# A decoder layer on one core: the feed-forward stage in seven products, its second matmul summed in PSUM

## The reference, cut to what matters

```
x = x + attention(layernorm(x), ...)         # block-sparse cache, 32 heads
x = x + cross_attention(layernorm(x), ...)   # 32 heads
x = x + ffn(layernorm(x), W1, b1, W2, b2)

def ffn(x, W1, b1, W2, b2):                  # x: 1024 x 512
    h = gelu(x @ W1 + b1)                    # W1: 512 x 2048, tanh form
    y = h @ W2                               # W2: 2048 x 512
    y = nan_to_num(y, nan=0, posinf=0, neginf=0)
    return y + b2
```

## Time and profile before

| | |
|---|---|
| median of three runs | 2126.07 us |
| the profiled execution, its span | 2129.9 us, 2128.0 us |
| granted clock over the span | 0.991 |
| feed-forward stretch (1935 to 2112 us), PE busy | 176.4 of 177 us |
| the same stretch, DVE, ACT, POOL | 127.5, 57.5, 44.6 us |

### The profile page before, as it was taken

The page is one execution under the profiler, slowest core; times in us unless marked ns, Lnnn a source line. Parts: engine busy times, 40 slices in busy tenths (PEclk is TensorE's granted clock), DMA queues, the critical chain, the costliest instruction groups (busy, mean ns, idle before and its releaser), DMA issues.

```text
span 2128.0 us, 33928 instructions
## 1 busy us (share of the span) xinstructions
PE 2076.8 (98%) x11620; PEld 1789.8 (84%) x11620; DVE 1500.9 (71%) x2365; ACT 1017.3 (48%) x2232; POOL 548.7 (26%) x428
## 2 busy tenths in 40 slices
PE   8999999999999999999899999999999999999996
PEld 7888888888888888888788888888888888877885
DVE  6777777777777777777766666666666666677776
...
DMA packets 44162, 76.90 MB, mean 36 GB/s; under 512 B 7378, under 2 KB 13650, under 8 KB 43602
## 3 DMA queue, kind: packets, MB, share of 16 engines
...
...
## 4 chain that ended last, share of the span: by engine, by line
PE 88%; DVE 6%; issue 3%; ACT 2%; DMA 1%; SPq 0%; DVEq 0%; ACTq 0%
PE bank L1087 22%; PE bank L1089 22%; PE bank L1088 22%; PE bank L1156 9%; PE bank L1202 6%; PE bank L1355 1%; PE bank L1354 1%; PE bank L1270 1%; PE bank L1271 1%; PE bank L1329 1%; DVE negmax L872 1%; DVE V_lo L866 1%; DVE xn L802 1%; DVE pT_lo L910 1%; DVE q_lo L904 1%
## 5 line engine op out<-in xcount | busy, mean ns | idle before, releaser
L882 DVE SCALAR_TENSOR_TENSOR xacc<-bank,rinv,xacc 128x512 f32<-128x512 f32 x512 | 375.7, 745 | 71.2 <-PE bank L1089 71.1
L481 ACT ACTIVATE pT_hi<-bank 128x512 fp32r<-128x512 f32 x320 | 190.8, 597 | 202.3 <-PE bank L1202 202.0
L872 DVE TENSOR_REDUCE negmax<-bank 128x1 f32<-128x640 f32 x256 | 210.2, 821 | 36.9 <-PE bank L1156 29.6
L535 ACT ACTIVATE prob<-bank,negmax 128x640 f32<-128x640 f32 x256 | 202.6, 791 | 66.2 <-DVE negmax L872 66.2
L910 DVE TENSOR_TENSOR pT_lo<-bank,pT_hi 128x512 fp32r<-128x512 f32 x320 | 217.5, 680 | 2.4 <-ACT pT_hi L481 2.4
L1202 PE MATMUL bank<-ident,prob 128*128 128x128 f32 x1280 | 191.3, 272 | 0.0
L1202 PEld LDWEIGHTS bank<-ident,prob 128*128 128x128 f32 x1280 | 159.2, 140 | 18.6
L378 POOL TENSOR_TENSOR wo_lo<-wo_raw,wo_hi 128x512 fp32r<-128x512 f32 x32 | 41.4, 1293 | 430.8 <-ACT wo_hi L481 430.8
L628 ACT ACTIVATE xprob<-xscore,negmax 128x128 f32<-128x128 f32 x256 | 99.5, 391 | 96.2 <-DVE negmax L963 96.2
L1087 PE MATMUL bank<-xwv_hi,cT_hi 128*128 128x256 f32 x512 | 143.4, 280 | 1.4 <-DVE xV_lo L930 1.4
L1088 PE MATMUL bank<-xwv_lo,cT_hi 128*128 128x256 f32 x512 | 143.1, 280 | 0.0
...
## 6 DMA issues: line engine op xcount, KB each, us to landing
wq_raw<-in_wq SPq DMA_DIRECT2D x32, 256.0 KB, 2.6
wo_raw<-in_wo SPq DMA_DIRECT2D x32, 256.0 KB, 2.6
xwv_raw<-in_xwv SPq DMA_DIRECT2D x16, 512.0 KB, 3.5
xwk_raw<-in_xwk SPq DMA_DIRECT2D x32, 256.0 KB, 3.5
xwq_raw<-in_xwq SPq DMA_DIRECT2D x32, 256.0 KB, 3.4
xwo_raw<-in_xwo SPq DMA_DIRECT2D x32, 256.0 KB, 2.6
w_raw<-in_w SPq DMA_DIRECT2D x32, 256.0 KB, 2.6
xacc<-in_x SPq DMA_DIRECT2D x8, 256.0 KB, 4.9
```

What stands on the lines that cost most here:

```text
L481: return s.activation(dst, src, ACT.Copy)
L535: s.activation(prob[:, slot, i, :].rearrange("p (a t) -> p a t", a=2), S_bank[i % 2], ACT.Exp, bias=negmax[:, slot, i:i + 1], scale=1.0, a ...
L872: v.tensor_reduce(negmax[:, slot, i:i + 1], S_bank[i % 2], mybir.AxisListType.XY, ALU.max, negate=True).then_inc(a["max"], 1)
L882: v.scalar_tensor_tensor(xacc[:, 4 * half + i, :], M, rinv[:, k, i:i + 1], xacc[:, 4 * half + i, :], ALU.mult, ALU.add).then_inc(sems["y"], 1)
```

## The change

**W1 by seven products.** The 512 inputs and the 1024 tokens are each cut in halves, W1's output blocks are taken in pairs (g, 8 groups: block 2g "first", 2g+1 "second"), and the 2 x 2 x 2 block product is made with seven products (P1 to P7) and sums of operands in place of eight. One product is 2 x 3 = 6 matmuls of 512 columns. P1 and P2 need only the first half of the tokens (`xB[0]`, `xB[1]`) and W1 itself (`we`, the early weights) and give, added, the hidden block 2g of the first half (c11). The other five need sums of the x quarters (`xS`, made on DVE in `xf`) and of the W1 quarters (`wl`, the late weights: four additions on POOL, `late_sums`; the five high parts in one copy of 1280 columns on ACT, `late_hi`; their low parts in one subtraction on DVE, `late_lo`). The results are combined on DVE: u2, u3, u4, then c12, c21, c22. `part` holds P1 (`p1_copy` on ACT). P1 and P2 run four groups ahead of the rest; groups 1 to 3 have them on banks 2 and 3, the others on 0 and 1.

**W2 by half.** For the first token half W2's products of all 16 blocks are summed in four PSUM banks (`y0`; 12 matmuls each, in whole or in two parts FIRST and LAST, in the order Y_ORDER). The second half's hidden values stay in `hid1` (16 x 512), and after the last group W2 is loaded once more (`again`, four buffers), split (`again_hi` on ACT; `again_lo` on DVE, every third on POOL), and the four tiles of the second half are done one after the other, each summing 16 x 3 matmuls in one bank. `yacc` is gone.

**Around it.** b2 is added to `xacc` by POOL after its last split of W2; `finish` makes the finite test and the sum on DVE straight from PSUM. W2's low parts are on DVE but for the first two. The first eight matmuls use only high parts. All loops are written out. The W1 and W2 semaphores reuse those of earlier stages (f_after). The buffers lie at fixed addresses.

```diff
@@ SP
+            def late_weights(g):
+                if g >= 2:
+                    sp.wait_ge(f["wlhi"], f0["wlhi"] + g - 1)
+                    sp.wait_ge(f["wllo"], f0["wllo"] + g - 1)
+                sp.dma_start(wl_f[g % 2][:, 0:4].rearrange("p (a s) c n -> p a (s c) n", a=2),
+                             w1[2 * g:2 * g + 2].rearrange("a p c n -> p a c n")).then_inc(s_wlraw[g % 2], 16)
+            def again(n):
+                if n >= 4:
+                    sp.wait_ge(f["ahi"], f0["ahi"] + n - 3)
+                    if (n - 4) % 3 == 2:
+                        sp.wait_ge(f["alo2"], f0["alo2"] + (n - 4) // 3 + 1)
+                    else:
+                        sp.wait_ge(f["alo"], f0["alo"] + n - 4 - (n - 4) // 3 + 1)
+                sp.dma_start(w2_again[:, n % 4], w2[n]).then_inc(s_x[n % 4], 16)
...
+            for g in range(NG):
+                for s_ in (7 + 2 * g, 8 + 2 * g):
+                    if s_ < NF:
+                        second(s_)
+                if g + 5 < NG:
+                    early(g + 5)
+                if g + 2 < NG:
+                    late_weights(g + 2)
+                if g == 4:
+                    sp.wait_ge(f["P2"], f0["P2"] + NG)
+                    for n in range(4):
+                        again(n)
+            for n in range(4, NF):
+                again(n)
@@ POOL
-            g.memset(yacc[:, :, :], 0.0).then_inc(s_y0, 1)
...
             pool.wait_ge(s_b, 16)
+            pool.wait_ge(L[3, "xn"], B)
+            for n in range(2, NF, 3):
+                pool.wait_ge(f["ahi"], f0["ahi"] + n + 1)
+                g.tensor_tensor(w2all_lo[:, n], w2_again[:, n % 4], w2all_hi[:, n], ALU.subtract)                 .then_inc(f["alo2"], 1)
             for b in range(B):
-                pool.wait_ge(L[3, "xn"], b + 1)
-                g.tensor_tensor(xacc[:, b, :], xacc[:, b, :], b2_sb[:, :], ALU.add).then_inc(s_xb, 1)
...
+                bias(b)
@@ ACT
+            for g in range(NG):
+                if g + 1 < NG:
+                    late_hi(g + 1)
+                for s_ in (5 + 2 * g, 6 + 2 * g):
+                    if s_ < NF:
+                        second_hi(s_)
+                if g + 4 < NG:
+                    p1_copy(g + 4)
+                if g + 1 == NG:
+                    hidden_late(g)
+                hidden_second(g, "c22", "g22", 2 * g + 1, late[:, 2])
+                if g + 4 < NG:
+                    hidden_early(g + 4)
+                if g + 5 < NG:
+                    early_hi(g + 5)
+                hidden_second(g, "c12", "g12", 2 * g, late[:, 1])
+                if g + 1 < NG:
+                    hidden_late(g)
@@ DVE
+            for g in range(NG - 1):
+                if g >= 4:
+                    late_lo(g + 1)
+                u2(g)
+                u4(g)
+                if g < 4:
+                    late_lo(g + 1)
+                u3(g)
+                c22(g)
+                for s_ in (5 + 2 * g, 6 + 2 * g):
+                    if s_ < NF:
+                        second_lo(s_)
+                if g + 4 < NG:
+                    c11(g + 4)
+                    h_lo(HALF_S[g + 4])
+                c12(g)
+                c21(g)
+                h_lo(LATE_S[g])
...
+            def finish(b, y):
+                if b >= 2:
+                    dve.wait_ge(f["fin"], f0["fin"] + b - 1)
+                v.tensor_scalar(finite[:, b % 2], y, 0.0, 0.0, ALU.mult, ALU.is_equal).then_inc(f["finite"], 1)
+                if b == 0:
+                    dve.wait_ge(s_xb, B)
+                v.tensor_tensor(ysum[:, b % 2], y, xacc[:, b, :], ALU.add).then_inc(f["sum"], 1)
+                dve.wait_ge(f["finite"], f0["finite"] + b + 1)
+                dve.wait_ge(f["sum"], f0["sum"] + b + 1)
+                v.copy_predicated(xacc[:, b, :], finite[:, b % 2], ysum[:, b % 2]).then_inc(f["fin"], 1)
...
+            for q in range(4):
+                hid1_lo_split(1, q)
+            for b in range(4):
+                finish(b, Y_bank[b])
+            for q in range(4):
+                hid1_lo_split(2, q)
+            dve.wait_ge(f["y1"], f0["y1"] + 1)
+            finish(4, Y1_bank[0])
...
@@ PE
+            for g in range(4):
+                fill = 3 if g == 0 else LATE_S[g - 1]
+                p6(g)
+                y0(fill, FIRST)
+                p5(g)
+                p1(g + 4)
+                p7(g)
+                p2(g + 4)
+                p3(g)
+                y0(fill, LAST)
+                p4(g)
+                y0(HALF_S[g + 4], EVERY)
+            p6(4)
+            for g in range(4, NG - 1):
+                p5(g)
+                p7(g)
+                y0(LATE_S[g - 1], FIRST)
+                p3(g)
+                p6(g + 1)
+                y0(LATE_S[g - 1], LAST)
+                p4(g)
...
+            for t_ in range(4):
+                for n in range(NF):
+                    if n % 4 == 0:
+                        pe.wait_ge(f["g1lo"], f0["g1lo"] + 4 * t_ + n // 4 + 1)
...
+                    last = mm3(Y1_bank[t_], [z[:, t_ % 2, n, :] for z in (hid1_hi, hid1_lo)],
+                               [z[:, n, :] for z in (w2all_hi, w2all_lo)], n == 0, n == NF - 1)
+                last.then_inc(f["y1"], 1)
```

More of the change, by code:

```diff
@@ L714, in _ @@
             ln_sqrt(3, 1)
[L715 removed]
+            for b in range(4):
+                x_first(b)
             ln_sqrt(3, 2)
[L718 to L724 removed]
@@ L742, in _ @@
-            f_step(0, 0)
-            with act.Fori(0, 6) as it:
-                for u in range(1, 5):
-                    f_step(it, u)
-            for u in range(1, 8):
-                f_step(6, u)
+            act.wait_ge(s_b1, 16 * NF)
+            s.activation(nrm[:, 4, 0:1], nrm[:, 1, 0:1], ACT.Gelu_apprx_tanh, bias=b1_sb[:, 0:1], scale=1.0)
+            late_hi(0)
+            p1_copy(0)
+            early_hi(3)
+            p1_copy(1)
+            hidden_early(0)
+            x_second(4)
@@ L1081, in _ @@
+            dve.wait_ge(f["y1"], f0["y1"] + 1)
+            finish(4, Y1_bank[0])
+            for q in range(4):
+                hid1_lo_split(3, q)
+            for b in range(5, B):
+                dve.wait_ge(f["y1"], f0["y1"] + b - 3)
+                finish(b, Y1_bank[b - 4])
         @block.tensor
@@ new lines, in y0 @@
+            def y0(s_, tiles):
+                if 0 in tiles:
+                    pe.wait_ge(f["hlo"], f0["hlo"] + s_ + 1)
+                    pe.wait_ge(f["w2lo"], f0["w2lo"] + s_ + 1)
+                for i in tiles:
+                    last = mm3(Y_bank[i], [z[:, s_ % 2, i * P:(i + 1) * P] for z in (hid_hi, hid_lo)],
+                               [z[:, s_ % 4, :] for z in (w2_hi, w2_lo)], s_ == 0, s_ == NF - 1)
+                if 3 in tiles:
+                    last.then_inc(f["y0"], 1)
```

630 lines of the change are left out of this document (468 added, 162 removed), and 3 rows, old and new, of the table f_after.

## The result

| | before | after |
|---|---|---|
| median, first comparison (four runs each) | 2126.21 | 2139.77 (2134.93 to 2143.48) |
| median, second comparison | 2127.46 | 2137.86 (2136.7 to 2140.96) |
| profiled execution, span | 2128.0 | 2141.5 |

The change is slower: ratio 1.0061, interval 1.0046 to 1.0077; the second time 1.0053, 1.0039 to 1.0068. The forecast was 2129 and the range ended at 2138; the second median lies just inside it, and the eight executions together have a median of 2139.2.

A forecast was written before the change was run, and what follows sets the result against it. The feed-forward stage was taken to run at PE's matmul rate. First product 1923.5, 168.0 of matmuls, waits, 3.2 of clock and a 5.3 tail summed to 2131.0, put as 2129 on the median; range 2112 to 2138.

The forecast's parts named there:

- the wait before tile 2: Second half of W2: tile 2's split stands on DVE behind finish and POOL's b2 adds; PE waits 7.0 us.
- lock: DVE and POOL block each other on shared ports; tile 1's splits and b2 adds add up, making tile 2's wait 8.1.
- P3's waits of 3 in groups 5 and 6 and 1 at group 7: PE waits for c22 before P3: 3.5 lost in groups 5 and 6, 1.0 in 7; groups 4 to 7 sum 9.7.
- the tail: After the last matmul, finish of one tile only: 5.3 us instead of 15.9.
- the first product: Head: PE's first product starts at 1923.5, 4.3 us earlier than before.
- Groups 0 to 3. Only P3 waits.: Groups 0 to 3: PE waits only at P3, 0.36 us each, 1.4 in all.
- none of over 0.5 in groups 1 to 3: Sign: no PE wait before P3 of over 0.5 us in groups 1 to 3.
- Group 4 loses 1.1.: Group 4: PE loses 1.1 us because POOL's sums come late behind the W1 load, as in group 5.
- The second half of W2: W2 reload through four buffers: PE ends tile 0 4.1 us late, then 0.5 for tile 1's first split.
- Clock. I take two falls: Two falls of PE's clock, one at tile 2 and one at group 5 or 6: 3.2 us (0 to 11).
- the 8 that I had named as a sign of being wrong: Sign: the prediction is wrong if the clock is low over more than 8 us.
- Rival 1: Clock falls at each long wait (head, groups 5 and 6, reload, tile 2): five falls, 11.0 us, 2137, slower; chance 0.20.

The follow-up runs named there:

- e6: Changed kernel with ACT's split of the early weights behind the two gelus of the late units instead of ahead: 2135.79 us.
- e10: Changed kernel with SP issuing each group's early and late weight loads ahead of the two W2 rows instead of behind: 2131.64 us.
- ep10: Changed kernel with e10's SP order, and PE doing all four W2 tiles ahead of P3 in groups 4 to 6: 2125.89 us.
- e4: Changed kernel with eight buffers instead of four for the second pass over W2: 2133.78 us.
- best2: Changed kernel with edits of e1, e2, e4, e6 and ep10, plus ACT's group 2 `p1_copy` ahead of `x_second(6)`: 2112.56 us.
- best3: best2 with POOL adding b2 ahead of the second pass over W2, and DVE making all sixteen `again_lo`: 2108.27 us.
- e0_again: The changed kernel run once more with no edit: 2137.86 us.
- e12: Changed kernel with the edits of e1 and e2 together: 2120.45 us.
- e1: Changed kernel with DVE splitting tile 2 of the second half before the finish of the first four tiles: 2130.36 us.
- e2: Changed kernel with DVE's split of the next late weights behind c22 instead of ahead of u2 in groups 4 to 6: 2128.38 us.
- e5: Changed kernel with filler matmuls on PE in the waits before P3 of groups 4 to 6 and before tile 2: 2133.89 us.
- e7: Changed kernel with POOL adding b2 ahead of its five W2 splits instead of behind them: 2129.45 us.

## Why the prediction was wrong

**What held.** The rate of the matmuls, the wait before tile 2 with its chain and its lock, P3's waits of 3 in groups 5 and 6 and 1 at group 7 (2.98, 3.03, 0.78), and the tail. Two sizes fit better than they deserve: the first product (1923.63 for 1923.5) came up to 3.8 us earlier in other executions, and the wait before tile 2 (6.73 for 7.0) was about 5.5 in seven. Of the lock, rows 11 do not show that "DVE began first": POOL's start is listed 0.01 us ahead. That POOL's adds stretch DVE's splits is shown by 6.88 against 2.49 us. The mechanism, in-order programs turning PE's saved work into waits, is shown: each wait went when the instruction in front of its releaser was moved, by what the timeline said.

**"Groups 0 to 3. Only P3 waits."** This step failed, by 4.4 us, and the sign "none of over 0.5 in groups 1 to 3" did too (1.23 and 1.51). P3 itself lost 0.27 in each of these groups, near the 0.36 forecast; what I had put at nothing is PE's wait for `hidden_lo`. It stands behind ACT's gelus, these behind ACT's split of the early weights, and that behind their load. I counted engine work and took each load as issued when its buffer is free. It is issued when SP's program comes to it, and that stood behind loads that wait for DVE. e6 (4.5 to 0.8 us in groups 1 to 3), e10 (none of these waits in groups 1 to 3) and ep10 (0.2 lost in each group) show it.

**"Group 4 loses 1.1."** It lost 2.75, from the same cause: with SP's new order alone the wait is gone. I had seen this for group 5 ("+0.6") and priced only the landing, 3.5, where 4.8 was the median.

**"The second half of W2", 4.1 and 0.5.** Mis-sized by 2.6. The round trip of four buffers was right as a mechanism (e4 saved 4.1), but with loads at 3.3 instead of 2.6, and I used the lock for tile 1 only. It is in tile 0 as well, since POOL splits every third row there: best2 loses 5.1 us in tile 0 with eight buffers and POOL's splits, best3 0.2 without these.

**"Clock. I take two falls", 3.2.** There were four in one execution and five in the other, 32 and 40 slow matmuls, 6.2 and 7.8 us. At 0.427 each, 32 of them are 13.7 us of low clock, over the 8 that I had named as a sign of being wrong. Rival 1 had the count, not the price: it put five falls at 11.0. Filling the waits gave 4.0 back (5.9 against the first median); of the rest, part can be slow matmuls that lay ahead of another wait, as at 2090 in e0_again. Rival 1's 2137 lay close to the result, but only 3 of the missing 10.5 us are the clock; the loads and the reload, which it lacks, are 9.4, less 1.9 elsewhere. That is agreement by chance in the larger part. The Trainium skill (TensorE: Matmul & The Clock Gate, "HAM oscillation — how this bites in real kernels") describes waits that bring the gate back time after time; that agrees with the three falls behind P3's waits and with the 0 slow matmuls of e12, though e0_again had none behind the second of its three, and I weighed it too low.

**The range.** Its upper end, 2138, took one error at a time. Three of the four terms that came out too low (groups 0 to 3, groups 4 to 7, the reload) share a cause, a time of issue or landing counted too early, and so went wrong together. The kernel before is also less steady than its first three runs: in later comparisons it went from 2124.7 to 2130.5.

**Open.** Why the clock falls behind one wait and not behind another of the same length: e0_again has three of 3.02 and falls behind the first and the third. What ends the 0.7 us "issue" wait at 1950: it is not listed in the six runs where the head has 6 or 7 slow matmuls and the banks are as in the change (e1, e2, e4, e5, e7, ep10), where PE comes some 1.4 us later and begins 0.6 later, so most of it is not PE's own. And no run has the seven products without the sum in PSUM, or the other way round: which of the two pays in best3 is not shown.
